# Residual image of a two-layer convolution kernel: added by TensorE into the filter's PSUM bank instead of by VectorE from a reloaded copy

## What is computed

```python
x = x + _L0_conv_ref(_gn(x), w0, w1, w2, bias)   # Haar wavelets, three 5x5 convolutions 128->128
x = x + _L1_conv_ref(_gn(x), spatial_weight)

def _L1_conv_ref(x, spatial_weight):             # 5x5 taps, patches by zero padding
    dot = einsum('bchw,bckhw->bkhw', x, patches)
    sim = dot / maximum(norm_x * norm_p, EPS)
    weight = (sim + 1) * 0.5 * spatial_weight
    return einsum('bckhw,bkhw->bchw', patches, weight)
```

## Time and profile before

| | |
|---|---|
| median of three runs | 2223.08 us (2222.95 to 2223.33) |
| the profiled execution | 2207.9 us, its span 2206.2 us |
| mean granted clock of TensorE | 0.850 |
| busy: PE, DVE, ACT, POOL | 1613.0, 1406.8, 740.0, 448.3 us |
| DVE's result additions, 128 of them | 47.9 us, 416 ns each |
| ACT's scaling of the copy, 32 | 39.6 us, 1237 ns each |
| wait of ACT for the copy (`x_res<-d_x`) | 96.2 us in 24 waits |
| HBM read, written | 238.70 MB, 86.61 MB |

### The profile page before, as it was taken

One profiled execution on the slowest core, in us unless ns is written; L12 is line 12 of the kernel. 1 busy time (PEld: TensorE's weight loads), 2 busy tenths in 40 slices (PEclk: granted clock), 3 DMA queues, 4 the chain that ended last, 5 costly groups with the idle time before them and its releaser, 6 DMA issues.

```text
span 2206.2 us, 49286 instructions
## 1 busy us (share of the span) xinstructions
PE 1613.0 (73%) x16895; PEld 853.4 (39%) x16895; DVE 1406.8 (64%) x2121; ACT 740.0 (34%) x1222; POOL 448.3 (20%) x792
## 2 busy tenths in 40 slices
PE   4776786778677786878668786878678786874465
PEld 3542343434333343434334343434334343432244
DVE  6427756866488456966478556966478445875354
ACT  2321243424243243423343243424243243423341
POOL 1343413012311213013311213012311113011000
PEclk8988997989888898979888897989888887987566
DMA  5243337673767547663766547673767448572665
GB/s 166 76 107 95 117 104 187 159 185 105 182 165 195 131 107 197 164 177 104 180 166 191 145 107 191 169 183 96 184 162 192 116 106 205 137 200 76 147 168 135
DMA packets 151105, 329.93 MB, mean 150 GB/s; under 512 B 47092, under 2 KB 96244, under 8 KB 150260
## 3 DMA queue, kind: packets, MB, share of 16 engines
q1 hardware_dynamic: 109296, 207.18, 36.9%
q0 software_dynamic: 41472, 118.24, 19.7%
HBM read 238.70 MB, written 86.61 MB: 147 GB/s over the span
## 4 chain that ended last, share of the span: by engine, by line
PE 29%; DMA 20%; SPq 19%; DVE 16%; issue 11%; ACT 3%; DVEq 1%; POOL 1%; ACTq 0%; POOLq 0%
DMA d_n<-st_n 11%; PE conv L1295 9%; DMA unit_mem<-d_n 8%; PE conv L1269 5%; SPq L410 5%; PE gram L1360 4%; SPq L384 4%; SPq L403 3%; PE out_ps L1382 3%; SPq L382 3%; PE conv L1254 2%; SPq L400 2%; PE stat_ps L1318 2%; DVE wgt L1017 2%; PE vals_ps L1343 2%
## 5 line engine op out<-in xcount | busy, mean ns | idle before, releaser
L1295 PE MATMUL conv<-thl,wconv 128*128 128x496 f16 (+2 forms) x1920 | 551.2, 417 | 23.9 <-DVE xa L896 12.5
L1017 DVE SCALAR_TENSOR_TENSOR wgt<-gram,tapw 124x512 f32<-124x512 f32 x512 | 350.0, 686 | 286.7 <-PE gram L1360 245.7
L468 POOL DMA_DIRECT2D ring<-in_x x576 | 333.7, 584 | 568.4 <-DVE bn L778 339.9
L1360 PE MATMUL gram<-unit_mem 128*60 128x128 f16 x4096 | 259.7, 253 | 221.9 <-DMA unit_mem<-d_n 128.2
L1360 PEld LDWEIGHTS gram<-unit_mem 128*60 128x60 f16 x4096 | 158.1, 117 | 444.8 <-issue 443.6
L1269 PE MATMUL conv<-thl,wconv 128*128 128x480 f16 (+7 forms) x1200 | 265.8, 377 | 0.0
L1295 PEld LDWEIGHTS conv<-thl,wconv 128*128 128x128 f16 x1920 | 169.4, 105 | 225.3 <-issue 73.2
L1318 PE MATMUL stat_ps<-st_n,sq_c 128*128 128x306 f32 x256 | 120.5, 560 | 170.0 <-ACT st_n L553 138.2
L1382 PE MATMUL out_ps<-wgt,vals 124*32 124x128 f32 x4096 | 194.6, 312 | 30.4 <-issue 24.4
L553 ACT ACTIVATE vals<-vals_ps 124x512 f32<-124x512 f32 x128 | 76.4, 597 | 363.3 <-PE vals_ps L1343 363.2
L1269 PEld LDWEIGHTS conv<-thl,wconv 128*128 128x128 f16 x1200 | 118.8, 101 | 132.0 <-issue 22.5
(11 more groups left out here) (133 smaller groups left out, 2057.8 us busy)
## 6 DMA issues: line engine op xcount, KB each, us to landing
unit_mem<-d_hl SPq DMA_DIRECT2D x128, 360.0 KB
unit_mem<-d_hl SPq DMA_DIRECT2D x256, 180.0 KB
ring<-in_x POOLq DMA_DIRECT2D x288, 128.0 KB, 3.3
ring<-in_x POOLq DMA_DIRECT2D x288, 127.0 KB, 3.6
d_hl<-st_hl SPq DMA_DIRECT2D x128, 180.0 KB
d_v<-st_v SPq DMA_DIRECT2D x128, 180.0 KB
unit_mem<-d_v SPq DMA_DIRECT2D x64, 360.0 KB
up<-d_z POOLq DMA_DIRECT2D x160, 128.0 KB, 3.2
```

Of the source, the lines that this page charges most:

```text
L468: pool.dma_start(dst, src).then_inc(raw_in[slot], 16)
L1017: V.scalar_tensor_tensor(out=dst, in0=g, scalar=SIM_SCALE ** 2, in1=tapw[:, :].unsqueeze(1).to_broadcast([KN, 2, 2 * QN]), op0=ALU.add, op ...
L1295: last = mm(dst[:, :, b0:b1], wconv0[:, w, 2 * (p % ROWS4) + s, dx + 2, :], thl[:, p % 2, d, s, :, b0 + dx:b1 + dx] if p % ROWS4 != 1 else ...
L1360: last = mm(bank[row:row + KQ, col:col + QN], key[:, q, e_at, TH * KW * g:TH * KW * g + KQ], tile[:, :, TH * g + 1:TH * g + 1 + TH, 1:1 + ...
```

## The change

PE adds the residual. Ahead of `filter_group(j, 0)`, at k = 4, it writes the whole bank `out_ps` with one product of a row of zeros (start), and adds 16 products of the identity, which DVE has scaled once by `unscale[0]`, with 4 rows x 32 columns of x1 in f32: for each band g and quadrant q one, into the 32 partitions of g. The filter's products now accumulate onto this. The mean enters as the bias of the copy from `out_ps` to `ostage`, which moves from DVE to ACT, ahead of `vals_out(j, 0)`. The stores of x1, `d_x1`, `x1_res`, its loads and its scaling are gone. DVE's `finals` waits until PE has read x1 (`res_read`) instead of until x1 was stored.

```diff
-            def load_residual(b, r):
-                sp.wait_ge(x1_saved[r], 16 * b + 16)
...
-                load_residual(b, 0)
                 save_half(b, 2)
...
                         store_band(b, u // 2 - 1)
-                        load_residual(b, u // 2)
...
-            def save_x1(n, r):
-                pool.wait_ge(x1_done, 4 * n + 2 * (r // 2) + 2)
...
-            def residual_in(b, r):
-                act.wait_ge(live_set, b + 2)
-                act.wait_ge(x1_res_in, 64 * (4 * b + r + 1))
-                part = x1_res[:, :, :, :].rearrange("p q h w -> p (q h w)")
-                copy(part, part, scale=unscale[0], bias=mean_ls).then_inc(res_ready, 1)
+            def result(b, u):
+                r, half = u // 2, u % 2
+                act.wait_ge(group_done, START + 4 * (8 * b + u + 1))
+                if u == 0:
+                    act.wait_ge(live_set, b + 2)
+                if half == 0:
+                    act.wait_ge(stored, START + 64 * (4 * b + r))
+                o = out_ps[:, :].rearrange("p (q h w) -> p q h w", q=Q, h=TH)
+                for rp in range(2):
+                    dst = ostage[:, rp:2 * TH:2, IMG // 2 * half:IMG // 2 * (half + 1)].rearrange("p h (w c) -> p c h w", c=2)
+                    last = copy(dst, o[:, 2 * rp:2 * rp + 2], bias=mean_ls)
+                last.then_inc(unit_out, 1)
...
                     if ls:
+                        if j > 0:
+                            result(b, j - 1)
                         vals_out(b, j, 0)
...
+                if ls:
+                    result(b, CONV_TILES - 1)
...
                 if not first(n):
                     dve.wait_ge(x2_done, 8 * (n - 1) + 6 + 2 * half)
-                    for r in (2 * half, 2 * half + 1):
-                        dve.wait_ge(x1_saved[r], 16 * n)
+                    dve.wait_ge(res_read, 8 * (n - 1) + 4 + 4 * half)
...
-                            if k == 2 and j > 0:
-                                result(b, j - 1)
...
+            V.memset(zero_row[:, :], 0.0)
+            V.tensor_scalar(ident, ident, unscale[0], None, ALU.mult).then_inc(gain_set, 1)
...
+            def residual(b, u):
+                r, half = u // 2, u % 2
+                pe.wait_ge(unit_out, START + 8 * b + u)
+                pe.wait_ge(x1_done, 4 * b + 4)
+                if u == 0:
+                    pe.wait_ge(gain_set, 1)
+                mm(out_ps[:, :], zero_row[:, :], wconv0[0:1, 0, 0, :, :].rearrange("p t o -> p (t o)")[:, 0:BANK], start=True, stop=False)
+                o = out_ps[:, :].rearrange("p (q n) -> p q n", q=Q)
+                for g in range(BANDS):
+                    row = BH * r + TH * g
+                    for q in range(Q):
+                        last = mm(o[C * g:C * g + C, q, :].rearrange("p (h w) -> p h w", h=TH), ident[:, C * q:C * q + C],
+                                  x1[:, row:row + TH, UW * half:UW * (half + 1)], start=False, stop=False)
+                last.then_inc(res_read, 1)
...
-                                  wgt[:, e % 2, g, c * QN:(c + 1) * QN], start=(c == 0), stop=(c == 1))
+                                  wgt[:, e % 2, g, c * QN:(c + 1) * QN], start=False, stop=(e == GROUPS - 1 and c == 1))
...
                             if k == 4:
+                                residual(b, j)
                                 filter_group(b, j, 0)
```

More of the change, by code:

```diff
@@ L182, in build @@
         unit_mem = sb("unit_mem", [P, 2, 3 * Q * FN], F16)
-        x1_res = sb("x1_res", [P, Q, TH, H0], F32)
         st_x2 = sb("st_x2", [P, 2, SH, SW], F32)
@@ L207, in build @@
         edge = sb("edge", [P, 1], F32)
+        zero_row = sb("zero_row", [1, P], F16)
         mix, average, same_quadrant, ident = (sq_c[:, n, :] for n in range(4))
@@ L242, in build @@
         d_z2, d_z1 = dram("d_z2", [B, P, H2 * H2], F32), dram("d_z1", [B, P, H1 * H1], F32)
-        d_x1 = dram("d_x1", [B, P, H0 * H0], F32)
         d_hl = dram("d_hl", [B, 2 * BANDS, 2, C, Q, FN], F16)
@@ L293, in build @@
         x1_done = sem("x1_done")
-        x1_saved = [sem(f"x1_saved{r}") for r in range(BANDS)]
         bn2_done = sem("bn2_done")
@@ L312, in build @@
         unit_in = [sem("unit_in0"), sem("unit_in1")]
-        x1_res_in = sem("x1_res_in")
-        res_ready = sem("res_ready")
+        res_read = sem("res_read")
+        gain_set = sem("gain_set")
         vt_ready = sem("vt_ready")
@@ L411, in load_unit @@
                                  norms[:, :, TW * e:TW * e + KW]).then_inc(unit_in[s], 16)
-            def load_residual(b, r):
-                sp.wait_ge(x1_saved[r], 16 * b + 16)
-                alone(sp)
-                sp.wait_ge(unit_out, START + 8 * b + 2 * r)
-                src = d_x1[b].rearrange("(q c) (h w) -> c q h w", c=C, w=H0)
-                for g in range(BANDS):
-                    row = BH * r + TH * g
-                    sp.dma_start(x1_res[C * g:C * g + C].rearrange("c q h w -> c q (h w)"),
-                                 src[:, :, row:row + TH, :].rearrange("c q h w -> c q (h w)")).then_inc(x1_res_in, 16)
             def store_band(b, r):
@@ L485, in raw_for_split @@
                     load_raw(batch, c, c % SLOTS)
-            def save_x1(n, r):
-                pool.wait_ge(x1_done, 4 * n + 2 * (r // 2) + 2)
-                pool.dma_start(d_x1[n, :, r * BH * H0:(r + 1) * BH * H0],
-                               x1[:, r * BH:(r + 1) * BH, :].rearrange("p h w -> p (h w)")).then_inc(x1_saved[r], 16)
             def load_up(i, n):
@@ L504, in iteration @@
             def iteration(i, nxt, conv, ls):
-                b = i - 1
-                if ls:
-                    save_x1(b, 2)
-                    save_x1(b, 3)
                 if conv:
@@ L527, in iteration @@
                     load_up(i, 2)
-                    save_x1(i, 0)
-                    save_x1(i, 1)
                     load_up(i, 3)
@@ L543, in _ @@
             pool.wait_ge(z1_saved, 16 * B)
-            for saved in x1_saved:
-                pool.wait_ge(saved, 16 * B)
             for saved in half_saved:
@@ L730, in iteration @@
                             half_in(b, j + AHEAD + 1)
-                        if j % 2 == 0:
-                            residual_in(b, j // 2)
                     if conv and j in (5, 6):
@@ L780, in set_live @@
             def set_live(i):
+                if not first(i):
+                    dve.wait_ge(unit_out, START + 8 * (i - 1))
                 V.tensor_copy(mean_ls, mean_conv).then_inc(live_set, 1)
@@ L1019, in weights @@
                     in1=tapw[:, :].unsqueeze(1).to_broadcast([KN, 2, 2 * QN]), op0=ALU.add, op1=ALU.mult).then_inc(wgt_done, 1)
-            def result(b, u):
-                r, half = u // 2, u % 2
-                dve.wait_ge(group_done, START + 4 * (8 * b + u + 1))
-                if half == 0:
-                    dve.wait_ge(res_ready, 4 * b + r + 1)
-                    dve.wait_ge(stored, START + 64 * (4 * b + r))
-                o = out_ps[:, :].rearrange("p (q h w) -> p q h w", q=Q, h=TH)
-                for rp in range(2):
-                    dst = ostage[:, rp:2 * TH:2, IMG // 2 * half:IMG // 2 * (half + 1)].rearrange("p h (w c) -> p c h w", c=2)
-                    ins = V.tensor_tensor(dst, o[:, 2 * rp:2 * rp + 2], x1_res[:, 2 * rp:2 * rp + 2, :, UW * half:UW * (half + 1)],
-                                          ALU.add)
-                ins.then_inc(unit_out, 1)
             def tap_weights():
@@ L1149, in iteration @@
                         tap_weights()
-                if ls:
-                    result(b, CONV_TILES - 1)
             def peak(n):
@@ L1231, in _ @@
             V.tensor_scalar(rel1, unscale[1], wscale[0], 0.5 * X_SCALE, ALU.mult, ALU.mult)
+            dve.wait_ge(wlevel_mm, 6)
+            V.memset(zero_row[:, :], 0.0)
+            V.tensor_scalar(ident, ident, unscale[0], None, ALU.mult).then_inc(gain_set, 1)
             dve.wait_ge(wfull, TILES_ALL)
@@ L1371, in gram @@
                 last.then_inc(gram_ready, 1)
+            def residual(b, u):
[12 more added lines that the diff above has]
+                last.then_inc(res_read, 1)
             def filter_group(b, u, e):
-                if e == 0:
-                    pe.wait_ge(unit_out, START + 8 * b + u)
                 pe.wait_ge(vals_done, START + 16 * b + 2 * u + e // 2 + 1)
```

## The result

The changed kernel takes **2241.55 us** (median of 7 runs), the kernel before 2218.92 in the same session: ratio 1.0105, 95% interval 1.0064 to 1.0146. The change makes the kernel about 1% slower, some 23 us; the forecast was 21 us faster.

The account below looks back on a forecast made before the run. No engine was full; the bound shifted from SP's queue to DVE (units 1 to 4), a load, then PE (units 6 and 7). Terms summed to -3.3 us an image, -21 us in all: 2202 us, range 2150 to 2245.

Parts of the forecast that it names:

- At nothing: Effects counted as zero, among them POOL's four stores an image: what stands behind them waits for ACT or DVE anyway.
- term 3: Units 1 to 4: DVE loses its additions, PE's products delay some grams; +0.8 us an image, ends -3.0 and +7.5.
- Term 1: Start of an image: copies into x1_res leave SP and its DMA queue, shortening PE's stall; -4.5 us, ends 2.1 and 8.5.
- term 2: PE's clock after the start's stall: a shorter stall leaves less work at the lower level; -1.5 us, ends 0 and -4.7.
- the second rival: Start: DMA is full with POOL's own transfers, so only the copies' issue comes free, -2.1; 2231 us, chance 0.15.
- Term 4: Units 6 and 7: PE has almost no cover for 2.0 us of products a unit; +3.5 us, ends +1.3 and +7.7.
- Visible weight loads: Residual products: each weight load stands in line with its product, 4.1 us a unit; 2282 us, chance 0.15.
- Term 5: End of an image: without DVE's additions after its last weights, the loop return begins earlier; -1.6 us an image.
- the lower end of 0.9: Low estimate of the products' cost a unit, in us: 0.65 for the filter's group of 16 plus 0.255 for the zero product.
- the first rival: Residual products with weight loads not hidden, 4.1 us a unit, slower; 2282 us, chance 0.15.
- three signs of being wrong: Residual groups of 3 us or more at clock 1.00; unit 1's stall near 8 us; filter's first group newly waiting.

Follow-up runs that it names:

- e2: Changed kernel with POOL holding an image's last copies into up and last four raw chunks until unit 6's load has landed: 2213.67 us, ratio 0.9978.
- e9: e2's wait moved behind the last copies into up, holding only the four raw chunks: changed kernel 2212.48 us (0.9970), kernel before 2195.86 us (0.9906).
- e11: Changed kernel with DVE's third addition of up moved two pairs of products later in unit 5: 2207.74 us, ratio 0.9955.
- e7: Kernel before without the stores to d_x1 and copies into x1_res (x1_res zero), additions and scaling kept: 2191.96 us, ratio 0.9886.
- e4: Changed kernel without the 16 residual products of a unit, zero product kept: 2179.78 us, ratio 0.9803.
- e1: Changed kernel with residual products reordered so neighbours write different groups of 32 partitions, and no zero product: 2180.71 us, ratio 0.9824.

## Why the prediction was wrong

**The step that failed is the one that is not there.** The prediction named unit 6's load as what sets the stage of unit 5, said that PE has slack there, and gave the stage no term; in before PE already stood 5.86 us for that load. Under "At nothing" it left out what stands behind the stores in POOL's queue, because it waits for ACT or DVE anyway, and did not ask how much sooner DVE would now let it go. Set beside the table of stages (means before rounding, us an image; the part of term 3 that is unit 1 lies in the first row):

| stages | term | forecast | measured |
|---|---|---|---|
| 0 and 1 | 1 and 2 | -6.0 | -2.7 |
| 2 to 4 | 3 | +0.8 | -1.1 |
| 5 | none | 0 | +4.8 |
| 6 and 7 | 4 | +3.5 | +3.5 |
| between | 5 | -1.6 | -0.15 |
| sum | | -3.3 | +4.2 |

Stage 5 is 4.8 of the 7.5 us and decides the sign. It is not the whole miss: without it the sum would be -0.5, and e2, e9 and e11, which take the meeting out of the changed kernel and leave its products in, come to 0.2 to 0.5% under before where the forecast was 0.9%. The rest is the start and the end, which gave less than their terms.

**What brings the meeting into every image.** The link was in the trace of before: two of seven images had the long form. DVE now reaches the third addition of up sooner. From the end of its last unit_lows to that addition (DVE's timelines, image 2) it is 11.6 us in before and 8.3 in after:

```profile
944.92 0.90 DVE L985 TENSOR_TENSOR st_hl<-st_b,st_hl 128x720 f16<-128x720 f32 x1
954.93 0.75 DVE L1031 TENSOR_TENSOR ostage<-out_ps,x_res 128x256 f32<-128x256 f32 x2
957.39 1.23 DVE L948 TENSOR_TENSOR xa<-up,xa 128x1024 f32<-128x1024 f32 x1
```

```profile
955.97 0.90 DVE L968 TENSOR_TENSOR st_hl<-st_b,st_hl 128x720 f16<-128x720 f32 x1
965.18 1.22 DVE L931 TENSOR_TENSOR xa<-up,xa 128x1024 f32<-128x1024 f32 x1
```

The same interval over images 0 to 6: in before 9.6 and 10.4 us in the two long images and 11.1 to 12.7 in the five short ones, in after 8.3 to 8.5 in all seven, in e11 11.7 to 13.3. Of the 3.3 us in image 2, 0.7 is the result's additions: e7, which keeps them and has no traffic, comes to 9.0 in its five long images. The other 2.6 come with the traffic gone. PE waited 3.10 us for unit 5's load in before and 1.20 in after (PE's timelines):

```profile
946.54 0.64 PE L1360 MATMUL gram<-unit_mem 128*60 128x128 f16 x8 [3.10 <-DMA unit_mem<-d_n]
```

```profile
955.96 0.47 PE L1327 MATMUL gram<-unit_mem 128*60 128x128 f16 x8 [1.20 <-DMA unit_mem<-d_n]
```

Behind that wait the clock was 0.76 from 950 to 960 us in before and 1.00 from 961 to 970 in after; how the shorter wait and the clock share the 2.6 us was not measured. These are gains that the change did make, and each moved POOL's transfers towards unit 6's load. e2, e9 and e11 show that the meeting is the cost, e7 that the traffic's absence alone brings it about in five of seven images.

**Term 1, the start: -4.5, with the clock's -1.5 in term 2.** Stages 0 and 1 shortened by 2.7 us together, 3.7 without the products (e4, and e7 alike). The term was too large, and the second rival, which gave the start 2.1, came nearer. It had the reason: the save stays stretched without the copies, at a DMA share of 0.98; unit 1's own load and the 16 raw transfers that POOL issues from 834.35 to 847.78 us stand around it. The clock's recovery was real (0.84 for 0.53).

**Term 3, units 1 to 4: +0.8.** Units 2 to 4 came out 1.1 us shorter together, inside the ends.

**Term 4, units 6 and 7: +3.5.** Measured +3.5 (0.9 and 2.6). The 2.0 us a unit were 2.6 in unit 7; unit 6 covered more. Visible weight loads did not come: the last residual records of unit 7, among those left out above, start at 1010.87, 1010.98 and 1011.09, 0.11 us apart, with loads of 0.113 us; a load in line with each record would put them some 0.22 apart.

**Term 5, the end: -1.6.** It came on DVE, and PE's clock took it back: -0.15 was left, -1.3 in e4. The prediction counted no clock there.

**The price of the products.** 2.0 us a unit at full clock was near the measured 2.18, but by luck. The earlier trace rows were read as one record for each product; the trace has two for an f32 product (last section), so the row of eight is four products and the filter's 16 are eight, and the lower end of 0.9 was misread in the same way. A second error, the overlap between groups of partitions put at 0.36, made up for the first. In the time of an image the prediction used two prices: the sum gives the products 4.3, with a part of DVE's gain in units 1 to 4 already set off, yet "each us of the products costs about five an image" stood in the first rival. By e1 and e4 against after, 1.7 and 2.3 us less a unit are worth 6.8 and 8.1 us an image, 4.0 and 3.6 per us: nearer to the rival's figure. What I took as covered in unit 1 and at the end was gain of the other terms that the products used up (1.8 and 1.2 us by e4). Without the products the change gains 3.9 us an image even with the long stage 5; the products cost 8.1.

**The forecast's form.** The range held the time, 2241.55 under 2245, by luck: it was drawn for dearer products, and what made the kernel slower was in none of the cases. Of its three signs of being wrong only one showed, and in part: the stall at unit 1 stayed at 7.6 us and more in three of seven images. None of them looked at unit 5.

## What to carry to other kernels

A stage that is long in two images of seven and short in five stands near a threshold. Before costing a change, find what its length turns on (here the start of one queue's bulk transfer against another queue's awaited load), and ask which way the change moves that. A gain that lets an engine off the path issue sooner can be a loss: price the meeting by bytes over the rate at which the full DMA engines move. And an awaited load should not stand in its queue behind a save that waits for something later: in the changed kernel that swap alone was worth four times the loss, in the kernel before 1.5%.

## What was not expected of the hardware

- The order of products by output partitions went with their rate. 32 records of 128 columns took 2.18 us, with the zero product ahead, where four quadrants followed each other into one group of 32 partitions, and 0.90 us where neighbours wrote different groups (e1): 0.028 us a record, though a record is 285 ns long in the mean in after and 289 in e1. Most of that overlaps. In e1 four neighbours also share their weights, but that is not needed: the filter's group, with other weights for each, runs as fast (16 records in 0.62 us).
- An f32 product of this form has two records in the trace: 2048 for the program's 1024. The row of eight in the earlier trace rows, from which the 2.0 us came, was therefore four products, and taken rightly it would have given 32 times 0.12, 3.9 us. That it was 2.2 is due to the overlap at the changes of partitions: in after the eight records into one group start 0.109 us apart, 0.87 us in all, but the next group starts 0.47 us behind the one before.
- The clock fell after a short stand at the end of full units: behind 23 us at 1.00 PE was idle for 3.18 us (row 996 to 1019 above), and the next four us ran at 0.50, its lower level. The length of the stand alone does not tell how far: in before 3.45 us of it were followed by four us at 0.68, in e4 3.16 us by 0.57.
